# One load of 1.5 MB an expert in place of two, in the expert feed-forward stage of a graph network kernel

## What is computed

```python
E, TOP_K = 64, 6                      # experts, experts of each token
topk_p, topk_i = jax.lax.top_k(softmax(x @ router_w.T + bias), TOP_K)
# expert_in[e]: the tokens that chose expert e, at most C = 234 of them
hg = jnp.einsum('ecd,efd->ecf', expert_in, w_gate)      # d 512, f 256
hu = jnp.einsum('ecd,efd->ecf', expert_in, w_up)
expert_out = jnp.einsum('ecf,edf->ecd', silu(hg) * hu, w_down)
# weighted by the gates and summed back to the tokens, plus a shared expert
```

## Time and profile before

| | us |
|---|---|
| median of 3 runs | 2389.14 (2387.55 to 2391.43) |
| the profiled execution, its own time | 2376.94 |
| its span | 2375.2 |
| expert loop, about | 700 to 1200 of the span |
| PE busy over the span | 2020.1 (85%) |
| DVE busy | 1337.3 (56%) |
| ACT busy | 1096.9 (46%) |

### The profile page before, as it was taken

How to read it: one execution, slowest core, us unless ns; L and a number is a source line. 1 busy time by engine, 2 the same in 40 slices (tenths; PEclk the granted TensorE clock), 3 DMA queues, 4 the chain that set the end, 5 groups by cost and what they waited for, 6 DMA issues and landing times. The chain is left out here.

```text
span 2375.2 us, 36495 instructions
## 1 busy us (share of the span) xinstructions
PE 2020.1 (85%) x10667; PEld 1501.1 (63%) x10667; DVE 1337.3 (56%) x1905; ACT 1096.9 (46%) x1732; POOL 681.5 (29%) x470
## 2 busy tenths in 40 slices
PE   5776799778949999999967679999999984899998
PEld 2455444255537777777756438999755544898997
DVE  6584377434226666766630425555411228999996
ACT  2462466121026666766630107777301115776674
POOL 3000200000764534544437127778200004000000
PEclk8897899877979999999989899999999998999999
DMA  2200780113037877877736238888400011000001
GB/s 89 78 1 1 202 276 11 38 58 124 2 92 251 282 242 254 294 269 267 270 116 170 86 96 202 205 202 205 167 0 1 0 79 81 1 1 1 0 0 44
DMA packets 118430, 282.55 MB, mean 119 GB/s; under 512 B 51264, under 2 KB 58426, under 8 KB 108542
## 3 DMA queue, kind: packets, MB, share of 16 engines
q1 hardware_dynamic: 50478, 189.25, 23.8%
q0 software_dynamic: 67792, 91.34, 13.7%
HBM read 242.05 MB, written 53.89 MB: 125 GB/s over the span
## 5 line engine op out<-in xcount | busy, mean ns | idle before, releaser
L1951 PE MATMUL ps<-ft,kw 128*128 128x125 f32 x2880 | 343.1, 279 | 37.0 <-DVE ft L1876 23.8
L1951 PEld LDWEIGHTS ps<-ft,kw 128*128 128x128 f32 x2880 | 331.1, 193 | 51.1 <-DVE ft L1876 30.7
L1122 POOL DMA_INDIRECT xg<-nrows,idx x128 | 245.0, 1914 | 264.7 <-PE ps L1148 232.5
L1445 POOL DMA_INDIRECT pg<-prows,srcI x170 | 214.3, 1261 | 55.3 <-issue 39.5
L1476 PEld LDWEIGHTS ps<-ehot,msg 125*128 125x128 f32 x1360 | 159.7, 193 | 11.6 <-issue 5.7
L1210 ACT ACTIVATE wh<-wexp 128x2048 fp32r<-128x2048 f32 x64 | 122.8, 1920 | 95.7 <-DVE gates L1266 62.2
L1476 PE MATMUL ps<-ehot,msg 125*128 125x125 f32 x1360 | 160.6, 277 | 6.6 <-ACT ehot L1568 5.4
L1900 ACT ACTIVATE ksq<-ksrc,kn 128x750 f32<-128x750 f32 (+2 forms) x144 | 116.5, 813 | 97.7 <-DVE cube L1859 97.7
L1820 POOL COPY ksrc<-nT 128x500 f32<-128x500 f32 (+1 forms) x10 | 10.8, 1075 | 520.9 <-SPq L1811 281.1
L1161 PE MATMUL ps<-wh,xh 128*128 128x512 f32 x364 | 151.0, 415 | 6.6 <-DVE xl L1285 6.6
L1272 DVE TENSOR_TENSOR wgl<-wexp,wh 128x2048 fp32r<-128x2048 f32 x64 | 146.6, 2291 | 2.2 <-ACT wh L1210 2.0
(11 more groups left out here) (276 smaller groups left out, 4072.3 us busy)
## 6 DMA issues: line engine op xcount, KB each, us to landing
wexp<-wexp_d SPq DMA_DIRECT2D x64, 1024.0 KB, 6.2
wexp<-wexp_d SPq DMA_DIRECT2D x64, 512.0 KB, 6.3
yrows<-y SPq DMA_DIRECT2D x91, 256.0 KB, 5.8
yrows<-nought POOLq DMA_DIRECT2D x1, 16384.0 KB, 57.1
attr<-attr_d SPq DMA_DIRECT2D x42, 250.0 KB, 5.5
kw<-kw_d SPq DMA_DIRECT2D x2, 4608.0 KB, 19.0
qs<-qk SPq DMA_DIRECT2D x32, 156.2 KB, 7.0
ks<-qk SPq DMA_DIRECT2D x32, 156.2 KB, 7.1
```

What stands on the lines that cost most here:

```text
L1122: pool.indirect_dma_start(xg[:, e % 2, h, :], None, d["nrows"], bass.IndirectOffsetOnAxis(ap=idx[:, 2 * e + h:2 * e + h + 1], axis=0), bou ...
L1445: pool.indirect_dma_start(pg[:, p % 4, t % 2, :], None, d["prows"], bass.IndirectOffsetOnAxis(ap=c.srcI[:, t:t + 1], axis=0)).then_inc(s_g ...
L1951: mm = pe.matmul(out[:, m * B:m * B + B], w[:, k, f, m * P:m * P + P], ft[:, f % RF, a:a + B], start=False, stop=False, skip_group_check=True)
```

## The change

The two loads of an expert become one of 128 partitions x 3072 floats, with one semaphore for each raw buffer. SP issues it after it has waited for both `s_glo` and `s_dlo`. ACT waits for the same semaphore before either conversion. The loads at the end of `routing` are joined in the same way.

```diff
-def routing(c, d, wexp, s_rgu, s_rdn, ahead):
+def routing(c, d, wexp, s_raw, ahead):
...
                 for q in range(WR):
-                    sp.dma_start(wexp[:, q, 0:WGU], d["wexp"][q, :, 0:WGU]).then_inc(s_rgu[q], 16)
-                    sp.dma_start(wexp[:, q, WGU:], d["wexp"][q, :, WGU:]).then_inc(s_rdn[q], 16)
+                    sp.dma_start(wexp[:, q, :], d["wexp"][q]).then_inc(s_raw[q], 16)
...
-                def load(e, part, s):
-                    sp.dma_start(wexp[:, e % WR, part], d["wexp"][e, :, part]).then_inc(s[e % WR], 16)
+                def load(e):
+                    sp.dma_start(wexp[:, e % WR, :], d["wexp"][e]).then_inc(s_raw[e % WR], 16)
 
                 for e in range(-1, NE):
                     if e + 1 + WR < NE:
                         sp.wait_ge(s_glo, e + 2)
-                        load(e + 1 + WR, GU, s_rgu)
                         sp.wait_ge(s_dlo, e + 2)
-                        load(e + 1 + WR, DN, s_rdn)
+                        load(e + 1 + WR)
...
                 def weights(e):
 
                     r, s = e % WR, e % WS
-                    act.wait_ge(s_rgu[r], 16 * (e // WR + 1))
+                    act.wait_ge(s_raw[r], 16 * (e // WR + 1))
...
                 def down_weights(e):
 
                     r, s = e % WR, e % WS
-                    act.wait_ge(s_rdn[r], 16 * (e // WR + 1))
+                    act.wait_ge(s_raw[r], 16 * (e // WR + 1))
```

More of the change, by code:

```diff
@@ L1033, in add, with experts @@
         self.eng.reg_mov(self.sums[name], self.eng.to_reg(self.sum(name, 0, 2 * NE) + self.count(e)))
-def experts(c, d, wexp, s_rgu, s_rdn):
+def experts(c, d, wexp, s_raw):
     nc = c.nc
@@ L1356, in feed_forward @@
         c.kidx = ctx.enter_context(nc.sbuf_tensor("kidx", [B, NB, TOPK], U32))
-        s_rgu, s_rdn = ([c.sem(f"ex_{n}{q}") for q in range(WR)] for n in ("rgu", "rdn"))
+        s_raw = [c.sem(f"ex_raw{q}") for q in range(WR)]
         wexp = ctx.enter_context(nc.sbuf_tensor("wexp", [P, WR, WEXP], F32))
@@ L1363, in feed_forward @@
             layernorm(c, "ln1_")
-            routing(c, d, wexp, s_rgu, s_rdn, ahead)
-        experts(c, d, wexp, s_rgu, s_rdn)
+            routing(c, d, wexp, s_raw, ahead)
+        experts(c, d, wexp, s_raw)
     c.renew()
```

## The result

| | before | changed |
|---|---|---|
| median of 6 runs, us | 2388.43 (2386.92 to 2393.45) | 2403.10 (2398.37 to 2406.63) |
| ratio to before | | 1.0055, 95% interval 1.004 to 1.007 |
| profiled execution, span | 2375.2 | 2404.9 |
| expert loop, first to last conversion of GU on ACT | 509.9 | 523.6 |

The changed kernel is slower: the medians differ by 14.7 us, and the ratio, 0.55%, comes to 13 us. The forecast was +4 us, called "within 0.2%" with a chance of 0.51; slower than that, which is what came, had 0.42. The direction and the range hold, the size does not.

The account below looks back on a forecast made before the run. PE was taken to bound double passes and a conversion chain without loads the single ones. Late loads +5 and gather time regained -1 gave +4 us on 2389.1, so 2393 us; range 2386 to 2405.

Parts of the forecast that it names:

- What bounds the stage: Expert loop: PE sets the pace in double passes; in single passes a conversion chain without loads makes the 6.06 us period.
- How long the joint load takes: Expert loop: about 7.8 us from issue at the head of a single-pass run, 8.0 to 9 inside one.
- The count of tight places: Expert loop: 21 of 61 loads have only 8.0 to 9.1 us; 14 come second or later, in 7 runs.
- ACT's waits: GU conversion in single passes: ACT waits for the joint load 5 to 12 times, 0.7 us per run, +5 us.
- late in full: Rival, ACT's wait for the joint load: each of 14 loads pays 1.1 us, +16 us, 2405; chance 0.15.
- What comes back: PE's 3.7 us of waits for gathered tokens in single-pass runs: late conversions give the gather time, -1 us.
- the gather suffers: Rival, gathers sharing engines with the load: PE's waits grow by up to 0.5 at 21 turns, +10, 2399; chance 0.12.
- the DMA engines save time: Rival, expert loads: one transfer with longer rows may occupy engines less, saving 3.7 us of gather waits, 2385.4; chance 0.13.
- A rule weighed: Joint load by the skill's fixed cost plus bytes: an estimated 5.6 us, never late, so the sum would be 0.
- SP: SP's issue of loads: 61 transfers fewer in the loop and 3 in routing, 0.33 us each, on a waiting engine: nothing.
- ACT's second wait: Conversion of DN weights: it waits for a semaphore already seen complete for the same expert: nothing.
- the first three loads: Loads issued in routing: the loop's start is held by routing's tables, not by weights: nothing.

Follow-up runs that it names:

- joint_xg3: Changed kernel (joint 1.5 MB load) with three buffers of gathered tokens in place of two; ratio to before 1.0027, loop 518.0 us.
- late_two: Kernel before with only the gate and up load's issue moved behind the second wait, still two loads and two semaphores; ratio 1.0001, loop 511.2 us.
- joint_wr4_xg3: Changed kernel with four raw weight buffers in place of three and three gathered-token buffers in place of two; ratio to before 0.9997, loop 508.0 us.
- three_wr4: Changed kernel with its load split by columns into three 512 KB transfers of 4 KB rows, and four raw buffers; ratio to before 0.9991, loop 507.6 us.
- joint_4k_wr4: Changed kernel, still one 1.5 MB transfer but with 4 KB rows, and four raw buffers; ratio to before 1.0026, loop 512.7 us.
- joint_wr4: Changed kernel with four raw weight buffers in place of three, rows still 12 KB; ratio to before 1.0045, loop 521.3 us.

## Why the prediction was right and wrong

**What bounds the stage: right.** Double passes kept their pace (10.88 us before, 10.90 after, mean), single passes lost. Past the start, the 35 single-pass periods of the loop had a mean of 6.16 us before and 6.52 after. That is 35 x 0.36 = 12.6 us, nearly all of the loop's 13.7.

**How long the joint load takes: right.** I had said 7.8 us at the head of a run and 8 to 9 inside one. The landing records of the changed kernel give a median of 7.9 in all, 7.4 at the head of a run and 8.2 inside one, with 9.7 the longest; for the joint loads of four other runs the profile has medians of 7.7 to 8.4. The room was 8.0.

The count of tight places was off. In the trace of before 23 loads have 8.0 to 9.1 us, not 21: the second issues at 1181.8 and 1187.9 us, behind the one taken for the last, have 8.0 and 8.1. Two loads or more in a row make 8 runs, not 7, and 13 loads come second or later, not 14. That changes the sum by less than 1 us.

**ACT's waits: the mechanism right, the loss less than forecast.** Forecast +5 us in 5 to 12 places. ACT waited 5.5 us in 4, and 5.8 in 4 on the other chip, but of this only 3.0 and 3.3 us are beyond the 0.63 us of idle time that these places have anyway. That they are so few was luck: the late gathers stretched the room from issue to conversion, from a median of 8.0 us in the 23 places to 8.8. joint_xg3, where the gather no longer does so, has 15 such waits, 9.5 us beyond the idle time, and a loop 8.1 us longer. So the load's term, taken by itself, was sized too low at 5, and the rival "late in full" (14 loads, 16 us) too high.

**"What comes back": this step failed.** I let the late conversions pay the gather back 1 us, and PE's waits for `xg` were not to rise above 3.7. The gather lost 7.8 us (2.0 to 9.8 from 710 us on), 5.9 on the other chip. The step assumed that the gather's own length stays as it is. It rose from 9.6 to 10.7 us, where single passes leave 10.3. In the kernel before, this is a gather's issue on POOL and the transposes of what it brought on PE:

```profile
760.10 2.24 POOL L1122 DMA_INDIRECT xg<-nrows,idx  x1 [1.74 <-PE ps L1148]
...
770.42 1.09 PE L1148 MATMUL ps<-ident,xg 128*128 128x128 f32 x8
```

By these medians a gather with 0.7 us to spare became one that is late by 0.4. In the sum, -1 should have been about +8.

**The rival "the gather suffers": the mechanism that decided**, with a chance of 0.12. Its price of up to 10 us was of the right size. It had two grounds, the new place of the load in time and its 12 KB rows. The first is refuted by late_two; the second is a part of it, and another part is that the load is one transfer. The rule that I had set beside it is the Trainium skill's, in "DMA: Bandwidth & Descriptors" (Queues, rings and completion order): each engine takes turns between queues by whole packets. The trace agrees as far as a gather lands later beside 12 KB rows (10.9 us) than beside 4 KB rows (10.0); the rule does not say why a single transfer of 4 KB rows is worse than three, and no run shows the turns themselves.

**The rival "the DMA engines save time": nothing was saved.** From 720 to 1180 us the two rows of a partition, 8 KB and 4 KB, took an engine 0.37 + 0.20 = 0.57 us in the kernel before (means); the one row of 12 KB took 0.58.

**"A rule weighed":** by the figures of the Trainium skill, in "DMA: Bandwidth & Descriptors" (Anatomy of one DMA), the joint load would have landed in an estimated 5.6 us and cost nothing. The skill has them from transfers that GpSimd issues, and these loads are issued by SyncE, which the prediction did not say. The measured medians of 7.7 to 8.4 us decide. In this loop a load shares the engines with the gather and the y store.

**SP, ACT's second wait, the first three loads:** nothing was found against their zero. SP's y store still follows 0.8 to 0.9 us behind the load's issue.

## What to carry to other kernels

Before merging transfers, list every other transfer that shares the DMA engines with them, and how much room each has before someone waits: the one that pays may be on another queue. Where two waits sit in the same chain, each hides the other's size, and idle time that was there before the change has to be taken off a wait before it is called a loss; take both causes away in one experiment to see what the change costs in all, and one at a time to see which comes first. If a merged load is wanted for other reasons, a buffer more on each side (joint_wr4_xg3) or column-wise pieces with a fourth buffer (three_wr4) made it free here.

## What the runs showed of the hardware that was not expected

- A gather on the software queue landed in 8.6, 10.0 and 10.9 us beside three transfers of 4 KB rows, one transfer of 4 KB rows, and one of 12 KB rows, all of the same 1.5 MB, issued behind the same two waits (three_wr4, joint_4k_wr4, joint_wr4); shortening rows from 4 to 2 KB brought only 0.1 us more.
- Two transfers of 64 partitions took twice the engine time for each 12 KB row (median 0.95 against 0.46 us) and made the whole kernel 4.8% slower.
- Rows of 12 KB used no less engine time than rows of 8 and 4 KB with the same bytes (0.58 against 0.57 us, means).
- Code that no run changed, the message passing stretch, took 269 to 272 us in the profiles of one chip and 293 to 299 on two others.
